# Layer 0's projections in a graph attention kernel: four of five pairs of node tiles by one level of Strassen's algorithm

## The reference, cut to what matters

```python
hs = (x @ Ws + bs).reshape(N, H, HD)      # x: 1250 x 768, Ws and Wd: 768 x 768
hd = (x @ Wd + bd).reshape(N, H, HD)
hs_e = hs[src]                            # 41250 edges gather rows of hs
e = leaky_relu(hs_e + hd[dst], 0.2)       # and meet the row of their destination
```

## Time and profile before

| | us |
|---|---|
| median of 3 runs (lowest, highest) | 2202.19 (2202.06, 2202.31) |
| profiled execution, its own time | 2200.64 |
| span of that execution, first to last instruction | 2198.9 |
| layer 0's turnover in it: first matmul to first matmul of the stage after | 372.61 to 539.12 |
| mean granted clock of PE, as a share of 2.4 GHz | 0.987 |

### The profile page before, as it was taken

How to read it: one execution, slowest core, us unless ns; L and a number is a source line. 1 busy time by engine, 2 the same in 40 slices (tenths; PEclk the granted TensorE clock), 3 DMA queues, 4 the chain that set the end, 5 groups by cost and what they waited for, 6 DMA issues and landing times. The chain is left out here.

```text
span 2198.9 us, 88044 instructions
## 1 busy us (share of the span) xinstructions
PE 2116.7 (96%) x31007; PEld 1709.3 (78%) x31008; DVE 1671.9 (76%) x4435; ACT 1134.6 (52%) x2749; POOL 980.8 (45%) x849
## 2 busy tenths in 40 slices
PE   7999999998999999999998899899999999999798
PEld 4665555555999999999997555699999999999676
DVE  5555882343899899898988764599999989999884
ACT  2111200023766676677665413476667667666584
POOL 0000011022677677677662311377767767766121
PEclk9999999999999999999999999999999999999899
DMA  6001144144888888888884124588888888888511
GB/s 197 1 0 53 35 126 145 58 129 117 237 254 254 254 251 255 247 258 253 255 255 140 62 89 136 142 255 252 255 254 252 253 255 253 253 253 252 179 70 50
DMA packets 143185, 400.58 MB, mean 182 GB/s; under 512 B 21811, under 2 KB 81625, under 8 KB 143073
## 3 DMA queue, kind: packets, MB, share of 16 engines
q0 software_dynamic: 59584, 298.64, 45.2%
q1 hardware_dynamic: 79691, 93.00, 13.4%
q10 hardware_dynamic: 3828, 7.85, 1.1%
HBM read 370.77 MB, written 17.17 MB: 176 GB/s over the span
## 5 line engine op out<-in xcount | busy, mean ns | idle before, releaser
L502 ACT ACTIVATE at_relu<-at_turned,ah_attn_size 128x512 f32<-128x512 f32 x1092 | 712.3, 690 | 380.2 <-PE at_turned L569 380.0
L483 POOL DMA_INDIRECT at_rows<-table,ah_index x360 | 441.9, 1227 | 205.0 <-DVE ah_index L709 99.7
L483 POOL DMA_INDIRECT ah_room<-table,ah_index x352 | 445.9, 1267 | 190.6 <-DVE ah_index L709 105.9
L699 DVE SCALAR_TENSOR_TENSOR sums<-sums,at_factor,at_total 128x97 f32 x1456 | 360.3, 309 | 25.9 <-issue 22.9
L565 PE MATMUL at_turned<-ident,ah_room 128*128 128x128 f32 x2208 | 341.9, 278 | 18.8 <-PEq L1665 18.8
L565 PE MATMUL at_turned<-ident,at_rows 128*128 128x128 f32 x2160 | 330.8, 276 | 0.0
L565 PEld LDWEIGHTS at_turned<-ident,ah_room 128*128 128x128 f32 x2208 | 243.8, 142 | 39.6 <-issue 39.6
L666 DVE SCALAR_TENSOR_TENSOR at_relu<-at_relu,ah_pair_sign 128x512 f32<-128x512 f32 x364 | 256.2, 745 | 0.0
L565 PEld LDWEIGHTS at_turned<-ident,at_rows 128*128 128x128 f32 x2160 | 236.0, 141 | 19.7 <-issue 19.7
L689 DVE TENSOR_TENSOR at_spread<-at_lined,at_weight 128x1024 f32<-128x1024 f32 x182 | 220.9, 1214 | 2.4 <-ACT at_weight L512 2.1
L569 PE MATMUL at_turned<-ah_place,dst_rows 96*128 96x128 bf16 x2208 | 216.1, 220 | 0.0
(11 more groups left out here) (318 smaller groups left out, 3125.1 us busy)
## 6 DMA issues: line engine op xcount, KB each, us to landing
at_flags<-run_flags SPq DMA_DIRECT2D x182, 64.0 KB
dst_rows<-pr_parts SPq DMA_DIRECT2D x76, 144.0 KB, 2.6
ah_place<-local_rows SPq DMA_DIRECT2D x92, 96.0 KB
at_place<-local_rows SPq DMA_DIRECT2D x90, 96.0 KB
table<-ah_room SPq DMA_DIRECT2D x20, 400.0 KB, 2.4
ah_room<-table,ah_index POOLq DMA_INDIRECT x368
at_rows<-table,ah_index POOLq DMA_INDIRECT x360
mx_w<-in_L_mix_W_qkv SPq DMA_DIRECT2D x4, 1152.0 KB, 11.7
```

What stands on the lines that cost most here:

```text
L483: pool.indirect_dma_start(rows[b][:, j, :], None, table, bass.IndirectOffsetOnAxis(index[b][:, j:j + 1], 0)).then_inc(gathered[b], 16)
L502: act.activation(relu[c][:], turned[chunk(b, c)][:], ACT.Relu, scale=attn_size[:, c:c + 1]).then_inc(bent, 1)
L699: dve.scalar_tensor_tensor(into[:, k], into[:, k], factor[b % 2][:, j, k:k + 1], part(j)[:, k, 0:HW], ALU.mult, ALU.add).then_inc(added, 1)
```

## The change

For layer 0, tiles 0 to 7 are taken as four pairs, tiles 8 and 9 (`ALONE_TILES`) stay as they are. A pair is a matrix of 2 x 2 blocks: two tiles, and two halves of the 768 inner features (three blocks of 128 each, HALF_C). The weight is cut likewise into 2 x 2 blocks of 384 x 384. One level of Strassen's algorithm in Winograd's form makes the pair from seven products ("pieces") in place of eight. A piece is three matmuls of the same 128 x 128 by 128 x 384.

The class `Halves` holds the new work. `sum_weights` makes four sums of weight blocks (twelve DVE instructions of 128 x 384 for each weight), `sum_nodes` four sums of node blocks for a pair (four DVE instructions of the same size); they lie in `dst_rows`, which is not yet in use. `multiply` is PE's part of a pair: seven pieces into four half banks a, b, d, e, in two sets used in turn (the second set lies in `moved_ps` and `turned`). a, b and d are used twice, so PE waits inside a pair for `piece_taken` to reach 1, 2 and 5 of its eight steps. `opening`, `middle`, `closing_two` and `closing_one` are DVE's part: ten additions of 128 x 384 for a pair where `add_bias` has four.

The order of the stage becomes: DVE first sums the source weights and the nodes of pair 0, while PE does `lone_product(0)` (tile 8), the transposition of the attention row, and `lone_product(1)` (tile 9). PE then waits until DVE has taken both, and does the source pairs 0 to 3, the destination pairs 0 to 3, and the two lone destination products. DVE sums the destination weights right after source pair 0. `turn_attn` moves between the two lone source tiles, the index copies and the first places stand ahead of destination pairs 0 and 2. `dst_row` gets a second buffer (`prod`), the stores and moves follow the new order of tiles, and POOL waits for `piece_done` where it waited for `product_done`.

The core of the diff:

```diff
+    def multiply(self, pe, side, pair, w):
...
+        if k > 1:
+            pe.wait_ge(self.piece_taken, STEPS * (k - 1))
+        piece(a, x11, w11)
+        pe.wait_ge(self.w_summed, side + 1)
+        pe.wait_ge(self.nodes_summed, pair + 1)
+        piece(b, s2, t2)
+        piece(d, s1, t1)
+        pe.wait_ge(self.piece_taken, STEPS * k + 1)
+        piece(a, x12, w21)
+        pe.wait_ge(self.piece_taken, STEPS * k + 2)
+        piece(b, s3, t3)
+        piece(e, x22, t4)
+        pe.wait_ge(self.piece_taken, STEPS * k + 5)
+        piece(d, s4, w22)
+
+    def opening(self, step, side, pair, offset):
...
+        dve.wait_ge(self.piece_done, PIECES * k + 1)
+        step(dve.tensor_tensor(self.first[:], a, offset[:, HALF:], ALU.add))
+        dve.sem_inc(self.piece_taken, 1)
+        dve.wait_ge(self.piece_done, PIECES * k + 2)
+        step(dve.tensor_tensor(self.second[:], b, self.first[:], ALU.add))
+        dve.sem_inc(self.piece_taken, 1)
+
+    def middle(self, step, side, pair, row_one, row_two):
...
+        step(dve.tensor_tensor(self.first[:], self.first[:], self.apart[:], ALU.add))
+        dve.wait_ge(self.piece_done, PIECES * k + 4)
+        step(dve.tensor_tensor(half_of(row_one, 0), by_rows(a), by_rows(self.first[:]), ALU.add))
+        dve.sem_inc(self.piece_taken, 1)
+        dve.wait_ge(self.piece_done, PIECES * k + 5)
+        step(dve.tensor_tensor(self.third[:], b, self.second[:], ALU.add))
+        dve.sem_inc(self.piece_taken, 1)
+        step(dve.tensor_tensor(half_of(row_two, 1), by_rows(d), by_rows(self.third[:]), ALU.add))
+        step(dve.tensor_tensor(self.second[:], d, self.second[:], ALU.add))
+        dve.sem_inc(self.piece_taken, 1)
+        step(dve.tensor_tensor(self.third[:], self.third[:], self.apart[:], ALU.add))
+        dve.sem_inc(self.piece_taken, 1)
...
@@ tensor
-                    for t in range(NT):
-                        product(t, w_src)
-                pe.wait_ge(dst_w_loaded, 16)
-                pe.wait_ge(attn_rows_loaded, 16 * KC)
-                pe.transpose(moved_ps[:, 0, 0:KC], ahead.attn_rows[:], ident[0:KC, 0:KC]).then_inc(attn_turned, 1)
-                for t in range(NT):
-                    product(NT + t, w_dst)
+                    lone_product(0, w_src)
+                    turn_attn()
+                    lone_product(1, w_src)
+                    pe.wait_ge(product_taken, len(ALONE_TILES))
+                    halves.multiply(pe, 0, 0, w_src)
+                    pe.wait_ge(attn_taken, 1)
+                    for pair in range(1, len(PAIR_TILES)):
+                        halves.multiply(pe, 0, pair, w_src)
+                pe.wait_ge(dst_w_loaded, 16)
...
+                    for pair in range(len(PAIR_TILES)):
+                        halves.multiply(pe, 1, pair, w_dst)
+                    pe.wait_ge(halves.piece_taken, STEPS * (2 * len(PAIR_TILES) - 1))
+                    lone_product(2, w_dst)
+                    lone_product(3, w_dst)
@@ vector
+                    halves.sum_weights(step, 0, w_src)
+                    halves.sum_nodes(step, 0)
...
+                    spare_sums(bias[0])
+                    source(0)
+                    turn_attn()
+                    dve.sem_inc(attn_taken, 1)
+                    source(1)
+                    dve.wait_ge(dst_w_loaded, 16)
+                    for pair in range(len(PAIR_TILES)):
+                        source_pair(pair)
+                        if pair == 0:
+                            halves.sum_weights(step, 1, w_dst)
+                    spare_sums(bias[1])
+                    halves.opening(step, 1, 0, bias[1])
...
+                    copy_index()
+                    destination_pair(0)
+                    destination_pair(1)
+                    first_places()
+                    destination_pair(2)
+                    destination_pair(3)
+                    lone_destination(0)
+                    lone_destination(1)
```

More of the change, by code:

```diff
@@ L1618, in turned_in, with half_of, by_rows @@
+def half_of(row, half):
+    return by_head(row[:, 0:D])[:, half * H // 2:(half + 1) * H // 2]
+def by_rows(ap):
+    return ap.rearrange("p (h g r) -> p h g r", h=H // 2, r=QUAD)
 def turned_in(turn):
@@ L1815, in product, with turn_attn, lone_product @@
                         for c in range(KC):
-                            last = pe.matmul(ps[i % 2][:, half, 0:HALF], buffer(i)[:, c // (KC // 2), c % (KC // 2)], w[:, c, half * HALF:(half + 1) * HALF],
+                            last = pe.matmul(ps[i % 2][:, half, 0:HALF], buffer(i)[:, c // HALF_C, c % HALF_C], w[:, c, half * HALF:(half + 1) * HALF],
+                                             start=c == 0, stop=c == KC - 1)
+                        last.then_inc(product_done, 1)
+                def turn_attn():
+                    pe.wait_ge(attn_rows_loaded, 16 * KC)
+                    pe.transpose(turned_attn, ahead.attn_rows[:], ident[0:KC, 0:KC]).then_inc(attn_turned, 1)
+                def lone_product(n, w):
+                    tile = node_t[ALONE_TILES[n % 2]]
+                    for half in range(2):
+                        for c in range(KC):
+                            last = pe.matmul(ps[n % 2][:, half, 0:HALF], tile[:, c // HALF_C, c % HALF_C], w[:, c, half * HALF:(half + 1) * HALF],
                                              start=c == 0, stop=c == KC - 1)
@@ L1863, in add_bias, with stored, linear_part @@
                     dve.sem_inc(product_taken, 1)
[L1865 to L1869, removed]
+                def stored(n):
+                    if n > 1:
+                        dve.wait_ge(row_stored[n % 2], 16 * (n // 2))
+                def linear_part(n):
+                    row = src_row[n % 2]
                     step(dve.tensor_tensor(prod[:], row[:, 0:D], attn_lin[:], ALU.mult))
@@ L1872, in source, with split_up @@
                     dve.sem_inc(row_ready, 1)
+                def source(t):
+                    stored(t)
+                    add_bias(t, src_row[t % 2], bias[0])
+                    linear_part(t)
+                def split_up(n):
+                    for s in range(SPLIT - 1):
+                        for half in range(2):
+                            dve.wait_ge(split_done, 2 * (SPLIT * n + s) + half + 1)
+                            rest = heads_half(dst_row_of[n % 2][:], half)
+                            step(dve.tensor_tensor(rest, rest, heads_half(parts[n % 2][:, s, :], half), ALU.subtract))
+                            dve.sem_inc(split_ready, 1)
@@ L1874, in destination @@
                 def destination(t):
                     add_bias(NT + t, dst_row, bias[1], (split_ready,))
[L1876 to L1881, removed]
@@ new lines, in destination_pair @@
+                def destination_pair(pair):
+                    at = 2 * pair
+                    if pair:
+                        dve.wait_ge(split_done, 2 * SPLIT * at)
+                    halves.middle(step, 1, pair, dst_row_of[1], dst_row_of[0])
+                    halves.closing_two(step, 1, pair, dst_row_of[0])
+                    dve.sem_inc(split_ready, 2)
+                    split_up(at)
+                    halves.closing_one(step, 1, pair, dst_row_of[1])
+                    dve.sem_inc(split_ready, 2)
+                    if pair + 1 < len(PAIR_TILES):
+                        halves.opening(step, 1, pair + 1, bias[1])
+                    split_up(at + 1)
@@ L1926, in _ @@
                 else:
+                    dve.wait_ge(ahead.w_loaded, 16)
+                    halves.sum_weights(step, 0, w_src)
+                    halves.sum_nodes(step, 0)
                     dve.wait_ge(bias_loaded, 32)
                     dve.wait_ge(attn_ready, 1)
[L1929 to L1942, removed]
+                    spare_sums(bias[0])
+                    source(0)
+                    turn_attn()
@@ new lines, in _, with copy_index @@
+                    dve.sem_inc(attn_taken, 1)
[7 more added lines that the diff above has]
+                    halves.opening(step, 1, 0, bias[1])
+                def copy_index():
+                    dve.wait_ge(fresh, 1)
+                    for b in range(UNROLL):
+                        dve.tensor_copy(ahead.index[b][:], rows_of(src_index, b)).then_inc(index_ready, 1)
```

141 lines of the change are left out of this document (129 added, 12 removed).

## The result

The changed kernel takes 2205.07 us (median of 20 runs, 2203.29 to 2208.73), the kernel before 2201.27 us (20 runs, 2199.40 to 2202.84): a ratio of 1.0018, 95% interval 1.0011 to 1.0025. That is 4.0 us longer, between 2.4 and 5.5. The forecast was 2207.0, which is 4.8 over the median then shown. That median, 2202.19 of three runs, lay 0.9 above the one of 20, so half of the 1.9 us between 2207.0 and 2205.07 is the starting value and not the change.

What follows compares the result with a forecast made beforehand. PE was taken to bound both passes: 4.35 + 1.15 + 4.0 + 6.3 + 0.4 + 4.2 = 20.4 us lost against 15.5 gained, 4.9 added to the median 2202.19, rounded down to 2207.0 us; range 2202.5 to 2211.

Steps and rivals of the forecast that it cites:

- The saving: Both passes on PE: 21 matmuls a pair in place of 24, eight pairs save 24 matmuls, 15.5 us.
- The attention row: PE idles before the attention transposition until six small DMAs land: 4.35 us lost, bounds 4.2 to 4.9.
- The banks: Before pair 0 PE waits until DVE has taken the second lone tile: 1.15 us lost.
- Inside a pair: PE's seventh piece waits for DVE's step 5: 0.5 us, eight times, 4.0 us lost, bounds 2.4 to 5.6.
- The destination weights: DVE's weight sums after source pair 0 delay the next pair's opening: PE stalls 6.3 us, bounds 6.0 to 7.0.
- The first places: Destination pass on DVE: their 0.85 us use up its 0.4 us of room once; 0.4 us lost, 0 to 0.9.
- The clock: PE at half clock after each of its two long stalls: 2.1 us each, 4.2 us lost, 5.3 at most.
- the clock that stays up: Rival: no half clock after PE's long stalls; 2204.9 us if it holds in one, 2202.8 in both; chance 0.14.
- the early attention row: Rival: the six DMAs land in about 3 us, PE idles 2.2 us without a clock fall; 2202.8 us; chance 0.08.
- the weight sums that stop nobody: Rival: DVE finishes the destination weight sums before PE wants the opening; stage 3.5 us shorter, 2198.7 us; chance 0.08.
- DVE as the bound of the destination pass: Rival: dearer signals and waits use up DVE's 0.4 us of room a pair; 2209.4 to 2210.2 us; chance 0.20.
- Free signals: Rival: a signal on DVE's chain inside a pair costs nothing; 0.9 us less, 2206.1 us; chance 0.08.

Runs made afterwards that it cites:

- the run with the sum ahead: Changed kernel with, in each pair, the addition of bank d to the second partial sum made before the wait for piece 5; 1.0006 to before.
- the run with the attention row moved: Changed kernel with the attention row's transposition between the two halves of the second lone source product; median 2199.13 us, 0.9993 to the kernel before.
- the other two edits: Attention transposition between the second lone source product's halves, and bank d's addition before the wait for piece 5; with sums on POOL, 2194.80 us.

## Why the prediction was right, point by point

The sum went by the stage, and the stage can be held against it term by term.

- *The saving.* 15.5 us. A pair without stalls takes 13.54 us in the run with the sum ahead, which is 21 matmuls at the old price. Right.
- *The attention row.* 4.35 forecast, 4.28 idle, which is 4.45 of PE's time with the records' 0.17. No row stands behind the 0.15 for waking in the forecast. With the row moved, this wait and its clock came back, 5.8 us.
- *The banks.* 1.15 forecast; 0.78 us of idle, 1.05 with the records' 0.17 and the exposed load.
- *Inside a pair.* This is the term that was mis-sized most: 0.5 each, 4.0 in all, against 0.34 and 2.7. I took 0.30 us from PE's end to DVE, read off the first half product behind the transposition. Its first record lasts 0.59 us in place of 0.49, so 0.10 of the 0.30 was an exposed weight load, which piece 5 has not: DVE starts 0.20 us after it (404.75 and 1.93, then 406.88). And I took 0.28 from DVE to PE at work, where 0.11 and an exposed load of 0.10 were measured. The value lay within the bounds of 0.3 to 0.7.
- *The destination weights.* 6.3 forecast; 6.22 idle, 6.4 by the starts and 0.1 of exposed load; gone when POOL does the sums.
- *The first places.* 0.4 forecast, nothing measured, and not for the reason given. I had put their 0.85 us on top of the 0.66 in which DVE waits for ACT's last copy. They stand in that wait, as the rows below show.
- *The clock.* 4.2 forecast, 3.7 measured. Both stalls did bring the fall, as the idles in the rows of before had. The size was partly chance: the same 6.2 us wait cost 2.1 us of clock in the changed kernel and 1.4 in the run with the attention row moved.

DVE around the first places (L2160), in the changed kernel:

```profile
483.34 0.56 DVE L1706 TENSOR_TENSOR pr_part<-pr_part,pr_apart 128x384 f32<-128x384 f32 x1 [0.65 <-ACT pr_parts L1903]
...
484.87 0.56 DVE L1711 TENSOR_TENSOR pr_part<-pr_moved_ps,pr_part 128x384 f32<-128x384 f32 x1 [0.38 <-PE pr_moved_ps L1675]
...
496.77 0.61 DVE L2160 TENSOR_SCALAR ah_place<-ah_place,split_of 96x512 bf16<-96x512 bf16 x2
...
498.74 0.56 DVE L1711 TENSOR_TENSOR pr_part<-pr_ps,pr_part 128x384 f32<-128x384 f32 x1 [0.30 <-PE pr_ps L1675]
```

In the pair before them DVE waits 0.65 us for ACT ahead of L1706, in this pair not at all. It still waits 0.30 us for PE's piece 5, where it waited 0.38.

With these the sum is 4.45 + 1.05 + 2.7 + 6.5 + 0 + 3.7 = 18.4 against 15.5: 2.9 us, where the stage shows 2.8. The forecast had 20.4.

The time of the program moved by 4.0 us (2.4 to 5.5), the stage by 2.8. The profiled span moved by 5.3. Of the rest 2.3 us lie in the last two stages, whose code is the same: layer 1's `attend` takes 662.4 us for 661.0 and `finish` 133.3 for 132.4. It isn't the change's: over the eight traces this `attend` takes between 661.0 and 663.5. And over the seven kernels compared with the one before, the time moved by 0.2 to 2.1 us away from what the stage did, for four of them up and for three down. What sets these few microseconds in a single run was not tried. So the forecast's 4.9 us met the measured 4.0 better than the stage's 2.8, and that part is luck.

The forecast said slower with 0.50 and no difference with 0.44. The ratio, 0.11 to 0.25% with 0.2% as the border, does not decide between them. With the stall inside a pair at its measured size the sum would have been 3.6 us, and no difference the likeliest case.

Of the rivals, the clock that stays up, the early attention row and the weight sums that stop nobody are refuted by rows. DVE as the bound of the destination pass is refuted for the changed kernel, where DVE still waits for PE in each pair, but narrowly: its round is 13.71 us (13.6 forecast) against PE's 13.88, so the room was 0.17 us and not 0.4. With the addition ahead of its wait it is the bound of the last two pairs. Free signals are refuted for these signals: from 408.18 to 408.89 the changed kernel's trace has 0.15 us between additions with a signal instruction, and 0.03 without (401.79 to 402.38). The page that the prediction sets against this, the Trainium skill's "VectorE: DVE Perf Modes", section "The DRAIN you can't avoid", measured a semaphore after each operation. The pairs with 0.03 us have such a one, each instruction waiting for the completion of the one before. So the row and the page don't differ, as the prediction had it; they speak of two kinds of signal.

## What to carry to other kernels

Strassen's step saved exactly its eighth of the paired tiles' matmuls, 15.5 us, and the profile says where more than that went: into waits at places to which work had been moved, and into the half clock behind them. PE's two long waits, 4.3 and 6.2 us, cost 1.6 and 2.1 us more than themselves, so the price of such a wait on a busy PE was the wait and the clock. A stall too short for the list of waits, 0.34 us a pair, cost another 2.7 us. And with 0.17 us of room in 14 on DVE the kernel gave back only part of what PE was spared: six of eight pairs got shorter, two didn't. Before giving one engine's sums to another, look at what both read: on POOL the weight sums were off the path and the kernel was 0.28% faster than before. With the other two edits it was no faster than that, until POOL's turn was put behind DVE's small instructions: then 0.56%.

## What the runs showed that I had not expected

POOL's elementwise sums and most of DVE's instructions with only SBUF inputs took turns. Beside POOL the 128 x 384 sums of DVE took 1.24 us in place of 0.56, the 128 x 8 ones 1.04 us in place of 0.26 to 0.28, and POOL's own 1.19 in place of 1.00; additions with one operand in PSUM stayed at 0.56, and the reduction by quads, which has one SBUF input, at 0.95. The Trainium skill's page "SBUF — State Buffer", section "Who interferes with whom", states that a DVE instruction with two SBUF inputs contends with a GpSimd instruction that reads SBUF, and that one with at most one such input outside the fast modes doesn't. The traces agree with the first by the sums of 1.24 us, and with the second by the additions of 0.56 and the reduction of 0.95. A TENSOR_SCALAR of 128 x 6 with one SBUF input did slow, from 0.17 to 1.60 us; whether it ran in a fast mode no trace shows.
